# X stored in 32 groups from within the full-size attention instead of after it

## What is computed

```python
def _attention(x):                       # B=4, C=128
    xf = x.reshape(B, C, H * W)
    scores = jnp.einsum('bcn,bcm->bnm', xf, xf)
    attn = jax.nn.softmax(scores, axis=-1)
    return jnp.einsum('bnm,bcm->bcn', attn, xf).reshape(B, C, H, W)
...
for scale in (4, 2, 1):
    block = _attention(_avg_pool(x, scale))
    out = out + jax.image.resize(block, (B, C, H, W), method='bilinear')
...
x = x + _L3_conv_ref(_gn(x))             # x is the result
```

## Time and profile before

| | us |
|---|---|
| median of 3 runs | 6086.92 (6082.94 to 6090.24) |
| profiled execution, device time | 6089.91 |
| its span in the trace | 6088.1 |
| mean granted TensorE clock | 0.941 |
| busy: TensorE, VectorE, GpSimd, ScalarE | 5080.5, 4895.2, 4801.2, 3385.0 |

### The profile page before, as it was taken

How to read it: one execution, slowest core, us unless ns; L and a number is a source line. 1 busy time by engine, 2 the same in 40 slices (tenths; PEclk the granted TensorE clock), 3 DMA queues, 4 the chain that set the end, 5 groups by cost and what they waited for, 6 DMA issues and landing times. The chain is left out here.

```text
span 6088.1 us, 72873 instructions
## 1 busy us (share of the span) xinstructions
PE 5080.5 (83%) x22486; PEld 2630.0 (43%) x22486; DVE 4895.2 (80%) x6700; ACT 3385.0 (56%) x4253; POOL 4801.2 (79%) x2227
## 2 busy tenths in 40 slices
PE   6888888888888888888888887972549989889897
PEld 2333333333333333333433434420326656566565
DVE  7999999999999999999999997005466676776665
ACT  4555565565566565555555552001437767677676
POOL 5999999999999999999999994002327767667676
PEclk8999999999999999999999998895879999999999
DMA  4565555556556555555555652681449999999999
GB/s 178 200 204 202 199 201 203 198 202 207 197 200 208 199 195 211 196 200 205 200 197 205 205 196 83 275 334 24 97 103 184 188 164 189 181 172 187 186 187 209
DMA packets 1424099, 1152.36 MB, mean 189 GB/s; under 512 B 1216730, under 2 KB 1226098, under 8 KB 1415796
## 3 DMA queue, kind: packets, MB, share of 16 engines
q1 hardware_dynamic: 1419384, 1148.31, 66.4%
q10 hardware_dynamic: 4478, 1.25, 0.2%
HBM read 814.23 MB, written 21.09 MB: 137 GB/s over the span
## 5 line engine op out<-in xcount | busy, mean ns | idle before, releaser
L871 POOL TENSOR_TENSOR mamba_state<-mamba_state,mamba_c_row 128x1024 f32<-128x1024 f32 x1024 | 2407.5, 2366 | 65.1 <-DVE mamba_state L831 57.6
L705 PE MATMUL mamba_y_ps<-mamba_state,ident 128*128 128x512 f32 x4096 | 1991.5, 612 | 42.7 <-POOL mamba_state L871 41.7
L1782 POOL TENSOR_TENSOR l3s_el<-l3s_s_sb,l3s_eh 128x1024 f16<-128x1024 f32 (+2 forms) x584 | 1169.1, 2012 | 709.7 <-ACT l3s_s_sb L1767 697.6
L831 DVE TENSOR_TENSOR_SCAN mamba_state<-mamba_decay,mamba_b_ps 128x1024 f32<-128x1024 f32 x704 | 1608.3, 2285 | 78.8 <-DVE mamba_b_ps L817 1.5
L705 PEld LDWEIGHTS mamba_y_ps<-mamba_state,ident 128*128 128x128 f32 x4096 | 780.3, 195 | 869.2 <-issue 681.2
L1790 DVE TENSOR_SCALAR_CACHE_REDUCE l3s_s_sb<-l3s_s_ps 128x512 f32<-128x512 f32 (+1 forms) x1096 | 752.7, 688 | 486.6 <-PE l3s_s_ps L1726 465.5
L1739 PE MATMUL l3s_o_ps<-l3s_vt,l3s_et 128*128 128x257 f16 x4368 | 879.1, 279 | 200.0 <-DMA l3s_et<-l3s_el 133.5
L1766 ACT ACTIVATE l3s_eh<-l3s_s_sb,l3s_shift 128x1024 f16<-128x1024 f32 (+2 forms) x584 | 634.6, 1087 | 548.9 <-DMA l3s_et<-l3s_el 448.8
L787 ACT ACTIVATE mamba_decay<-mamba_dt,mamba_A 128x1016 f32<-128x1016 f32 x704 | 791.7, 1133 | 234.8 <-POOL mamba_dt L852 168.7
L817 DVE TENSOR_TENSOR mamba_b_ps<-mamba_dtu,mamba_b_ps 128x1024 f32<-128x1024 f32 x704 | 849.8, 1207 | 28.3 <-PE mamba_b_ps L693 27.9
L693 PE MATMUL mamba_b_ps<-mamba_bc,mamba_pick 128*128 128x512 f32 x1408 | 572.4, 489 | 282.3 <-DVE mamba_state L831 275.6
(11 more groups left out here) (304 smaller groups left out, 5226.9 us busy)
## 6 DMA issues: line engine op xcount, KB each, us to landing
mamba_c_row<-mamba_c_rows SPq DMA_DIRECT2D x1024, 512.0 KB, 3.8
mamba_b_row<-mamba_c_rows SPq DMA_DIRECT2D x320, 512.0 KB, 4.8
l_ring_a<-in_L_conv_W SPq DMA_DIRECT2D x28, 1024.0 KB, 11.0
l2b_ring_b<-in_L_conv_W SPq DMA_DIRECT2D x26, 1024.0 KB, 11.0
mamba_xs<-X SPq DMA_DIRECT2D x64, 256.0 KB, 5.5
l_ring_a<-in_L_conv_W SPq DMA_DIRECT2D x14, 704.0 KB, 12.7
l2b_ring_b<-in_L_conv_W SPq DMA_DIRECT2D x13, 704.0 KB, 12.7
l_ring_a<-in_L_conv_W SPq DMA_DIRECT2D x14, 640.0 KB, 12.1
```

What stands on the lines that cost most here:

```text
L705: last = nc.tensor.matmul(y_ps[:, half(h)], C["ident"][:, :], state[:, s % STATES, half(h)], start=False, stop=(s == S - 1))
L831: nc.vector.tensor_tensor_scan(state[:, s % STATES, :], by, add, 0.0, ALU.mult, ALU.add).then_inc(s_scan, 1)
L871: nc.gpsimd.tensor_tensor(state[:, s % STATES, :], state[:, s % STATES, :], c_row[:, s % C_ROWS, :], ALU.mult).then_inc(s_hc, 1)
L1782: nc.gpsimd.tensor_tensor(el[:, part, off:off + EXPW], s_sb[:, par, j * EXPW:(j + 1) * EXPW], eh[:, part, off:off + EXPW], ALU.subtract).t ...
```

## The change

`attend` and `attention` get the output as an argument, and SyncE's program in the full-size attention stores X in 32 groups of four tiles: 512 columns of the 128 partitions, 2 KB in each, 256 KB a group. Group g is issued at tile 4g + 11 (i % 4 = 3), ahead of its transposes, behind waits for the group's four updates and for its band; the last two groups are issued behind the last transposes. A last wait stands for all 32. `store_x` and its block are gone.

```diff
@@ attention, SyncE's program
+                def store_group(g):
+                    b, k = divmod(g, QT // 4)
+                    mine = slice(k * 4 * P, (k + 1) * 4 * P)
+                    wait(sp, s_x, 4 * (g + 1))
+                    wait(sp, s_band, 4 * (g + 1))
+                    sp.dma_start(store[b].rearrange("t n f -> t (n f)")[:, mine],
+                                 X[:, b * PIX + k * 4 * P:b * PIX + (k + 1) * 4 * P]).then_inc(s_store, 16)
+
                 if full:
                     load_small(0)
                 for b in range(B):
                     for i in range(QT):
+                        if full and i % 4 == 3 and b * QT + i >= 8:
+                            store_group((b * QT + i) // 4 - 2)
                         if full and i % 4 == 1 and b * QT + i + 4 <= B * QT:
                             load_small((b * QT + i) // 4 + 1)
...
+                if full:
+                    for g in range(B * QT // 4 - 2, B * QT // 4):
+                        store_group(g)
+                    sp.wait_ge(s_store, 16 * (B * QT // 4))
...
-def store_x(nc, sem, X, out):
-    s = sem("x_stored")
-    with nc.Block() as block:
-        @block.sync
-        def _(sp):
-            for b in range(B):
-                sp.dma_start(out[b].rearrange("t n f -> t (n f)"), X[:, b * PIX:(b + 1) * PIX]).then_inc(s, 16)
-            sp.wait_ge(s, B * 16)
...
-        attend(nc, sem, "l3", X, C, scale_g, bias_g)
-        store_x(nc, sem, X, out)
+        attend(nc, sem, "l3", X, C, scale_g, bias_g, out)
```

More of the change, by code:

```diff
@@ L1498, with attend @@
 SHIFT_UP = 10.0
-def attend(nc, sem, tag, X, C, scale_g, bias_g):
+def attend(nc, sem, tag, X, C, scale_g, bias_g, store):
     n2, n4 = PIX // 4, PIX // 16
@@ L1513, in attend @@
         keep(nc, sem, tag, kept, result)
-    attention(nc, sem, f"{tag}s1", C, PIX, None, (X, scale_g, bias_g, kept), None)
+    attention(nc, sem, f"{tag}s1", C, PIX, None, (X, scale_g, bias_g, kept, store), None)
 def keep(nc, sem, tag, kept, result):
@@ L1621, in attention @@
         if full:
-            X, scale_g, bias_g, kept = full
+            X, scale_g, bias_g, kept, store = full
             xn = m.sb("xn", [P, W])
@@ L1668, in attention @@
         s_small = sem(f"{tag}_small_loaded")
+        s_store = sem(f"{tag}_x_stored")
         s_part2 = sem(f"{tag}_half_size_rows_begun")
```

## The result

| | before | changed |
|---|---|---|
| median in the first comparison, us | 6083.39 (6 runs, 6081.58 to 6090.24) | 6065.24 (6 runs, 6061.47 to 6072.40) |
| profiled execution, its span | 6089.91, 6088.1 | 6063.67, 6061.9 |

The ratio is 0.9966 with a 95% interval of 0.9956 to 0.9976: 20.7 us less, between 14.6 and 26.8. Forecast were 19.1 us less and 6067.8, counted from a median of three runs before, 6086.92; with six runs that median is 6083.39. The 7.0 were not forecast, and have a cause of their own.

What follows compares the result with a forecast made beforehand. A loop of latencies was taken to bound the attention, with 21.7 us of tail behind it and no compute engine busy. 6086.92 - 19.1 at the end + 0 in the loop gave 6067.8 us, range 6063 to 6087.

Steps and rivals of the forecast that it cites:

- The end: Tail after the last update of X: 21.67 us shrink to 2.54, so the change gives 19.1 us.
- release: Tail, from the last update of X to the last group's store: 0.1 us.
- landing: Tail, the last 256 KB store: 1.45 us fixed plus 0.61 of data at 428 GB/s, 2.1 us.
- remainder: Tail, from the last store's landing to the span's end: the same 0.34 us as before.
- the loop's term: Thirty stores inside the attention loop: 0 us added, never below nothing, upper bound 18.3 us at 428 GB/s or 36 at 218.
- Step (b): SyncE's time in the loop: about 2.6 us of slack against 0.6 to 1.2 us of issue; cost 0.
- Step (c): DMA time in the loop: 0.61 to 1.2 us per store fits in 1.4 us of holes per tile; cost 0.
- Step (d): Small loads (138 KB, 1.01 us) already issued in such a place at i % 4 = 1 cost nothing visible; so 0.
- main risk: In the loop, a write to memory might behave between transposes otherwise than the small reads do.
- Rival A: DMA engines bound the attention: 18.3 us return in the loop, 6086.1, chance 0.12; mild form 6071 to 6077, 0.08.
- Rival B: In the loop, each store keeps the rings until landed: 2.1 us per group, 63 in all, 6131 us; chance 0.08.
- Rival C: SyncE reaches group 30 or 31 late, so the tail would stay; chance 0.01.

Runs made afterwards that it cites:

- the two copies: Changed kernel with each of the thirty loop stores followed by one more of the same columns into a spare tensor; 0.9986 of the kernel before, step 11.87 us.
- four copies: Changed kernel with each of the thirty loop stores followed by three more of the same columns into a spare tensor; 6136.91 us, 1.0073 of the kernel before.

## Why the prediction was right, and where it wasn't

**The end.** Right in every term: release 0.05 (0.1 forecast), landing 2.0 (2.1), remainder 0.4 (0.34), together 2.45 against 2.54. The way to the landing, the fixed part from a larger copy in the same direction plus bytes at the measured rate, was better than the nearest copies of the same size (3.2 and 5.5), and than the Trainium skill's price for the GpSimd path in "DMA: Bandwidth & Descriptors", section "Anatomy of one DMA", which gave 2.6.

**The step that failed** is the loop's term, 0 with a floor: "below nothing it can't be: nothing in the loop gets lighter". The price of the stores was looked for, and anything else that the edit does to the loop was put at nothing without a row for it. In the profiles the attention went from 1548.3 and 1546.7 us to 1541.3 and 1540.9, 5 to 7 less, and the last update stood 7.0 us earlier than before, where the prediction had it within 2. An unused semaphore does the same to the kernel before (1540.4), and the change with its semaphore allocated last does not (1546.3). So the term is 0 from the stores and about 5 less from the shifted semaphores; why the numbers matter is open. The sum is then 19.2 + 5 = 24 us, which is within the measured 20.7 (14.6 to 26.8) and 21.9 (14 to 30). That 19.1 lies so near 20.7 is luck in part: the interval of the medians is wider than the missing term, and the profiled pair, 26.2 apart, shows the whole.

**The stores in the loop, cost 0.** Right in value: 11.38 and 11.36 over a store against 11.37 in a kernel that has none there. The working was partly wrong. Step (b) counted SyncE's two idle times as 2.6 us of slack for an issue of 0.6 to 1.2. The store's issue (0.78) did fit into the first, but the eh issue behind it grew too, by 0.85, and left 0.6 of the second. I counted SyncE and the DMA engines as two separate budgets, (b) and (c), while the length of an issue ties them together. Step (c)'s 1.4 us of usable holes comes out at about 0.85. One store of 0.67 fits in either; twice as much does not, as the two copies show.

Step (d)'s test case pointed to the right value, but not by the same way. The small loads leave the eh issue behind them as it is (median 1.79 us with them, 1.79 to 1.80 in the other tiles of the kernel before), and a store makes it 0.85 longer. So a write between the transposes did behave otherwise than the small reads, which the prediction had named as its main risk; whether direction or size makes the difference is not shown. It stayed free because 0.6 us of slack were left, and that much the prediction had not worked out.

**Rival A**, the DMA engines as the bound, is false for one store per tile: double the bytes in two tiles cost nothing, although the DMA share reads 1.00. From the second 256 KB in one place on bytes do cost time, by way of SyncE's issues. **Rival B**, a store that holds the queues until it lands, is false: four copies, whose landings would be some 8 us, lengthen the step by 1.8. The Trainium skill's rule of 1 MiB or more per DMA ("DMA: Bandwidth & Descriptors", "Rules for kernel authors"), named beside it, is turned round here: 1 MB groups are about 18 us slower than 256 KB groups. **Rival C** didn't occur.

## What to carry to other kernels

Here, work that left the kernel's tail for a loop was free as long as it fitted a hole at each place: find the loop that sets the step in the chain of waits, put the transfer ahead of an instruction that isn't in it, and make it as large as one hole takes, even where the average DMA share reads full. Look at the issue behind the new transfer: when its duration grows until the next issue follows at once, the hole is used up, and spreading over more places helps where merging hurts. And when a change leaves a few microseconds that no step explains, try the side effects of its text, such as semaphores allocated in between, as a kernel of their own.

## What the runs showed of the hardware

- One unused semaphore allocated per attention shortened the landings of a transpose by about 0.1 us in every second tile (4.54 to 4.43) and the kernel's time by 7.3 us (1.8 to 12.8).
- A transposing issue on SyncE (eh, part 0) takes 1.8 us in the median without a store, 2.65 behind a store of 256 KB, 3.3 and 3.6 behind two and four, and 5.0 behind one of 1 MB. Behind two small loads (138 KB, from memory) it stays at 1.8.
- The issue of a 256 KB store took 0.33 us when nothing had been issued for over a microsecond, 0.78 in the median of the loop and 0.68 in a row of 32.
- After 3.01 us in which TensorE stood idle, a 128x512 float16 matmul went from 0.38 to 0.63 us, and the granted clock of the 12 us read 0.72; the second long steps of the four-copy kernel follow this clock in all 23 groups. After idle times of 2.34 to 2.71 us the clock fell in ten groups and stayed in nine.
